# GpSimd mixes the rows for v and r of a time-mixing layer, and TensorE multiplies them once

## The reference

```
xs = jnp.pad(x, ((0, 0), (1, 0), (0, 0)))[:, :-1]        # the row of one step earlier
xk = x * time_mix_k + xs * (1.0 - time_mix_k)
xv = x * time_mix_v + xs * (1.0 - time_mix_v)
xr = x * time_mix_r + xs * (1.0 - time_mix_r)
K, V, R = xk @ Wk.T, xv @ Wv.T, xr @ Wr.T
wkv = _wkv(W, U, K, V)                                    # a scan over the 256 steps
output = (jax.nn.sigmoid(R) * wkv) @ Wo.T
```

## Time and profile before

| | us |
|---|---|
| time, median of 3 runs | 412.81 (411.13 to 414.19) |
| the profiled execution | 414.23 |
| its span | 412.2 |
| TensorE busy with matmuls | 353.9 |
| VectorE busy | 283.1 |
| ScalarE busy | 234.3 |
| GpSimd busy | 186.0 |

### The profile page before, as it was taken

One profiled execution on the slowest core, in us unless ns is written; L12 is line 12 of the kernel. 1 busy time (PEld: TensorE's weight loads), 2 busy tenths in 40 slices (PEclk: granted clock), 3 DMA queues, 4 the chain that ended last, 5 costly groups with the idle time before them and its releaser, 6 DMA issues.

```text
span 412.2 us, 6923 instructions
## 1 busy us (share of the span) xinstructions
PE 353.9 (86%) x2435; PEld 219.1 (53%) x2435; DVE 283.1 (69%) x669; ACT 234.3 (57%) x417; POOL 186.0 (45%) x339
## 2 busy tenths in 40 slices
PE   6869999899999999999888989797885587999930
PEld 2444545466475755747464756363633353788820
DVE  5694676774958669485985477789887864455633
ACT  2756796857759497585537334959757440333300
POOL 4001635747283562897561402500039107777750
PEclk9868999999999999999999999999998766999985
DMA  8400000000000000000000001900010011455346
GB/s 231 125 0 2 2 0 2 1 2 2 2 0 2 2 0 2 2 2 0 2 2 0 2 0 40 338 3 1 0 57 0 0 53 25 108 154 153 97 137 204
DMA packets 18035, 18.07 MB, mean 44 GB/s; under 512 B 2937, under 2 KB 14234, under 8 KB 17746
## 3 DMA queue, kind: packets, MB, share of 16 engines
q1 hardware_dynamic: 14930, 12.91, 10.6%
q0 software_dynamic: 1440, 2.90, 2.7%
q10 hardware_dynamic: 1632, 1.84, 1.3%
HBM read 12.12 MB, written 5.62 MB: 43 GB/s over the span
## 4 chain that ended last, share of the span: by engine, by line
PE 58%; DVE 15%; ACT 12%; issue 6%; DMA 4%; POOL 3%; POOLq 0%; ACTq 0%; DVEq 0%
PE at_av L258 9%; PE at_sim L241 8%; PE at_misc L278 6%; PE mo_y L2028 6%; PE at_misc L207 5%; PE mo_h L2016 4%; PE at_misc L202 4%; ACT at_attn L462 3%; PE at_misc L222 3%; DVE at_attn L615 2%; PE at_misc L271 1%; ACT at_sq_v L440 1%; PE mi_yf L1059 1%; PE at_sim L1059 1%; DVE ah_lm_stats L1121 1%
## 5 line engine op out<-in xcount | busy, mean ns | idle before, releaser
L615 DVE TENSOR_TENSOR at_attn<-at_sim,at_attn 128x1024 f32<-128x1024 f32 x64 | 75.3, 1218 | 41.8 <-ACT at_attn L462 41.4
L462 ACT ACTIVATE at_attn<-at_sim 128x1024 f32<-128x1024 f32 x64 | 62.2, 1029 | 36.8 <-PE at_sim L241 36.4
L766 POOL TENSOR_TENSOR at_osq<-at_ob 128x512 f32<-128x512 f32 x32 | 35.1, 1100 | 67.5 <-ACT at_ob L470 66.9
L258 PE MATMUL at_av<-at_attn,at_v_raw 128*64 128x256 f32 x512 | 64.1, 393 | 0.4 <-DVE at_v_raw L606 0.4
L258 PEld LDWEIGHTS at_av<-at_attn,at_v_raw 128*64 128x64 f32 x512 | 34.6, 139 | 25.2 <-issue 8.7
L1273 POOL TENSOR_SCALAR mi_at_lane<-mi_raised_lanes,mi_lane_of,mi_number 128x128 f16<-128x128 f32 x20 | 18.8, 955 | 58.0 <-DVE mi_lane_of L1786 58.0
L241 PE MATMUL at_sim<-at_q,at_k 32*128 32x256 f32 x512 | 41.1, 410 | 4.1 <-DVE at_attn L615 2.2
L2067 ACT ACTIVATE mo_hT<-mo_h,mo_b 128x320 f32<-128x320 f32 x32 | 16.3, 528 | 37.6 <-PE mo_h L2016 23.3
L207 PE MATMUL at_misc<-at_w_kv,at_xnT 128*128 128x512 f32 x64 | 33.9, 629 | 2.4 <-ACT at_sq_v L440 2.2
L241 PEld LDWEIGHTS at_sim<-at_q,at_k 32*128 32x128 f32 x512 | 25.3, 188 | 18.9 <-issue 9.3
L278 PE MATMUL at_misc<-at_w_out,at_ob 128*128 128x128 f32 x256 | 30.1, 276 | 0.0
(11 more groups left out here) (305 smaller groups left out, 677.5 us busy)
## 6 DMA issues: line engine op xcount, KB each, us to landing
mo_w<-in_L_ffn_w SPq DMA_DIRECT2D x16, 256.0 KB, 3.0
mo_answers<-mo_zero SPq DMA_DIRECT2D x2, 1024.0 KB, 8.9
mo_got<-mo_answers SPq DMA_DIRECT2D x6, 256.0 KB, 4.4
mo_rows<-ro_rows SPq DMA_DIRECT2D x4, 276.0 KB, 2.3
at_w_kv<-in_L_attn_Wkv ACTq DMA_DIRECT2D x1, 640.0 KB, 4.6
x_res<-in_L_attn_tokens SPq DMA_DIRECT2D x2, 256.0 KB, 6.1
at_w_out<-in_L_attn_Wout SPq DMA_DIRECT2D x1, 512.0 KB, 9.2
mo_b<-in_L_ffn_b SPq DMA_DIRECT2D x1, 512.0 KB, 4.8
```

The lines of the kernel that those rows point to most:

```text
L258: last = mm(av[e * DV:(e + 1) * DV, half * T:(half + 1) * T], v_raw[b % 2][:, j, h * DV:(h + 1) * DV], attn[(2 * Q + half) % 4][:, e, j, : ...
L462: nc.scalar.activation(attn[n % 4][:, :, :, :].rearrange("p e j t -> p e (j t)"), sim[half][:, :, :], ACT.Relu).then_inc(relu_ready, 1)
L615: v.tensor_tensor(r, sim[half][:, :, :], r, ALU.mult).then_inc(attn_ready, 1)
L766: g.tensor_tensor(osq[b % 2][:, 2 * n:2 * n + 2, :], o, o, ALU.mult).then_inc(osq_ready, 1)
```

## The change

For chunks 0 to 2, v and r are mixed before the multiplication: GpSimd subtracts the earlier rows from the rows (`step`), multiplies the difference by the mixing factor of the channel, and adds the earlier rows, for v and then for r, into the SBUF tiles `mixed_v` and `mixed_r`. TensorE multiplies each mixed tile once by the unmixed weights, and waits for `mixed_ready` first. Chunk 3 goes on as before, and k in all chunks. The unmixed weights of v and r therefore stay in place, and their mixed version goes to new tiles `w_new`. GpSimd's list gets the mixing of chunk 0 ahead of the blanks, of chunk 1 behind the ones, and of chunk 2 behind the constants. GpSimd waits for the chunk's rows (`xwT_ready`), and before it overwrites a mixed tile for the projection that read it (`v_done`, `r_done`); it waits for its own instructions through `link` where one reads what the one before wrote.

```diff
--- before.py
+++ after.py
@@ -861,6 +861,7 @@
 
 MIN_P = -1e38
 MIX = ("k", "v", "r")
+MIXED = ("v", "r")
 
 
 class WkvInputs:
@@ -872,6 +873,7 @@
 
         self.w = {m: sb("w_" + m, [P, P]) for m in ("k", "v", "r", "o")}
         self.w_old = {m: sb("w_old_" + m, [P, P]) for m in MIX}
+        self.w_new = {m: sb("w_new_" + m, [P, P]) for m in MIXED}
         self.ident, self.minus = sb("ident", [P, P]), sb("minus", [P, P])
         self.cols, self.keep = sb("cols", [P, 5]), sb("keep", [P, 3])
         self.minus_u = sb("minus_u", [P, 1])
@@ -896,7 +898,8 @@
             g.tensor_scalar(self.w_old[m][:, :], self.w[m][:, :], self.keep[:, n:n + 1], None, ALU.mult).then_inc(self.prepared, 1)
         pool.wait_ge(self.prepared, 6)
         for n, m in enumerate(MIX):
-            g.tensor_scalar(self.w[m][:, :], self.w[m][:, :], self.cols[:, 2 + n:3 + n], None, ALU.mult).then_inc(self.prepared, 1)
+            own = self.w_new[m] if m in MIXED else self.w[m]
+            g.tensor_scalar(own[:, :], self.w[m][:, :], self.cols[:, 2 + n:3 + n], None, ALU.mult).then_inc(self.prepared, 1)
 
 
 EXPERTS, EXPERT_HIDDEN, CAPACITY = 8, 512, 320
@@ -1187,7 +1190,10 @@
 
 
         w, w_old, minus, cols, minus_u = wkv.w, wkv.w_old, wkv.minus, wkv.cols, wkv.minus_u
+        w_new = wkv.w_new
         decay, xwT = ahead.decay, ahead.xwT
+        step = sb("step", seq)
+        mixed = {m: sb("mixed_" + m, seq) for m in MIXED}
         pp = sb("pp", [P, NB, T + 1])
         sums = sb("sums", [P, 2, NB, T + 1])
         u = [sb(f"u{i}", seq) for i in range(4)]
@@ -1252,7 +1258,7 @@
         mask_ready, counts_done, routed, meta_ready = sem("mask_ready"), sem("counts_done"), sem("routed"), sem("meta_ready")
         above_ready, lanes_ready, last_lanes, found = sem("above_ready"), sem("lanes_ready"), sem("last_lanes"), sem("found")
         centred, rwc_ready = sem("centred"), sem("rwc_ready")
-        chain = sem("chain")
+        chain, pool_chain, mixed_ready = sem("chain"), sem("pool_chain"), sem("mixed_ready")
 
         def formed(c):
 
@@ -1298,9 +1304,27 @@
             g.memset(eps[:, :], LN_EPS).then_inc(consts, 1)
             g.memset(pp[:, :, 0:1], MIN_P).then_inc(consts, 1)
             g.memset(sums[:, :, :, 0:1], 0.0).then_inc(consts, 1)
+            link = Chain(pool, pool_chain)
+
+            def mix(c):
+
+                now, before = xwT[c % 2][:, :, 1:T + 1], xwT[c % 2][:, :, 0:T]
+                pool.wait_ge(xwT_ready, c + 1)
+                link(g.tensor_tensor(full(step), now, before, ALU.subtract))
+                for m, used in zip(MIXED, (v_done, r_done)):
+                    n = MIX.index(m)
+                    if c:
+                        pool.wait_ge(used, c)
+                    link(g.tensor_tensor(full(mixed[m]), full(step), cols[:, 2 + n:3 + n].unsqueeze(2).to_broadcast(seq), ALU.mult))
+                    g.tensor_tensor(full(mixed[m]), full(mixed[m]), before, ALU.add).then_inc(mixed_ready, 1)
+
+            pool.wait_ge(wkv.prepared, 9)
+            pool.wait_ge(ahead.prepared, 3)
+            mix(0)
             moe.make_blanks(g)
             g.memset(ones[:, :], 1.0).then_inc(consts, 1)
             g.memset(one_row[:, :], 1.0).then_inc(consts, 1)
+            mix(1)
             pool.wait_ge(moe.consts_loaded, 16 * 9)
             g.tensor_scalar(centring[:, :], moe.ident[:, :], -1.0 / P, None, ALU.add).then_inc(consts, 1)
             g.tensor_copy(tri[:, :], moe.tri32[:, :]).then_inc(consts, 1)
@@ -1311,6 +1335,7 @@
             g.tensor_scalar(number[:, :], tokens[:, :], 1.0, None, ALU.add).then_inc(consts, 1)
             g.tensor_copy(rows[:, :, TOKEN], tokens[:, :]).then_inc(consts, 1)
             pool.wait_ge(consts, 13)
+            mix(2)
             for r in range(FINAL):
                 pool.wait_ge(routed, r + 1)
                 for k in range(2):
@@ -1349,8 +1374,15 @@
                 ahead.transpose_f(pe, c, xt)
 
             def project(m, c, dst):
+                now = w_new[m] if m in MIXED else w[m]
                 mm(by_batch(dst), w_old[m][:, :], xwT[c % 2][:, :, 0:T], start=True, stop=False)
-                return mm(by_batch(dst), w[m][:, :], xwT[c % 2][:, :, 1:T + 1], start=False, stop=True)
+                return mm(by_batch(dst), now[:, :], xwT[c % 2][:, :, 1:T + 1], start=False, stop=True)
+
+            def project_mixed(m, c, dst):
+                if c == LAST:
+                    return project(m, c, dst)
+                pe.wait_ge(mixed_ready, 2 * c + MIX.index(m))
+                return mm(by_batch(dst), w[m][:, :], full(mixed[m]), start=True, stop=True)
 
             def project_k(c):
                 pe.wait_ge(wkv.prepared, 9)
@@ -1368,12 +1400,12 @@
                 pe.wait_ge(xwT_ready, c + 1)
                 if c:
                     pe.wait_ge(v_used, c)
-                project("v", c, v_bank).then_inc(v_done, 1)
+                project_mixed("v", c, v_bank).then_inc(v_done, 1)
 
             def project_r(c):
                 if c:
                     pe.wait_ge(rw_ready, c)
-                project("r", c, r_bank).then_inc(r_done, 1)
+                project_mixed("r", c, r_bank).then_inc(r_done, 1)
 
             def gate(c, k, bank):
                 pe.wait_ge(ahead.xfT_ready, c + 1)
```

## The result

| | before | changed |
|---|---|---|
| median of 9 runs each, us | 412.19 | 416.67 |
| ratio, 95% interval | 1 | 1.0099 (1.0063 to 1.0136) |
| profiled execution, us (span) | 414.23 (412.2) | 416.67 (414.7) |

What follows compares the result with a forecast made beforehand. It took TensorE's chain of waits, with v's projection on it twice, as the bound, VectorE about a microsecond behind in chunk 1. Terms 3.9 + 1.7 + 0.95 = 6.55 on 412.8 gave 419.4 us, range 413.9 to 423.5.

Steps and rivals of the forecast that it cites:

- The mechanism: Chunk 1: GpSimd's mixing and VectorE's two-SBUF-operand instructions wait for each other whole, making total 4.7 us late.
- the starved GpSimd: Rival: VectorE keeps GpSimd out until chunk 1's total ends, v is mixed late, 3.4 us lost, 416.2; chance 0.13.
- within 1%: Outcome class 408.7 to 416.9 us: first rival, most of the second and the forecast's low end; chance 0.27.
- a VectorE that isn't held: Rival: GpSimd's reads leave VectorE room, the 1.5 us come out, 411.3; chance 0.12.
- the clock that stays low: Rival: TensorE's clock stays low through chunk 2's down projection or the routing, 9 us and more; chance 0.15.
- GpSimd's price: Each 128x512 mixing instruction takes 1.27 us, 1.13 after a wait; low end 1.04.
- the count for the low end: Chunk 1 with 1.04 us per GpSimd instruction, step going first: total 3.45 late; sum 2.75, 415.6 us.
- the signs: Chunk 1's scans, past and total each 1.7 to 2.3 us, total ending near 271, clock under 1.00 between 270 and 280.
- What is late next: Behind chunk 1's total, ScalarE's copy of the transposed rows comes late, so TensorE's gate matmul starts 3.9 us later.
- The clock: Gate matmul and subtraction run at 1.2 instead of 2.4 GHz: 1.7 us more, from 0 to 2.69 beyond that.
- Chunk 2: r's addition waits under scaled, then holds q; rw ends late, so the chain's addition starts 0.95 us late.
- What the change removes: Six fp32 matmuls in chunks 0 to 2, two on the chain: 0.86 and 0.62, together 1.5 us if nothing else moved.

Runs made afterwards that it cites:

- experiment 4: Kernel before, with chunk 1's five mixing instructions added as GpSimd memsets of a spare tile, TensorE waiting for them and projecting twice: 410.25 us, ratio 0.9975.
- 1: Changed kernel with GpSimd still mixing and TensorE waiting, but v and r again projected with two matmuls by the scaled weights: 416.55 us, ratio 1.0084.
- experiment 7: Changed kernel with chunks 1 and 2 mixed in VectorE's gaps and their v projected later on TensorE; run twice: 410.48 and 410.86 us, ratio 0.9963 both times.
- the second of 8: Version with mixing in VectorE's gaps and v projected later, but v and r projected with two matmuls as in the kernel before: 412.19 us, ratio 1.0007.
- experiment 3: Three runs, each mixing only one chunk on GpSimd, the others as in the kernel before: chunk 0 411.31, chunk 1 418.01, chunk 2 413.84 us.
- chunk 2 alone: Only chunk 2 mixed on GpSimd and multiplied once, chunks 0 and 1 as in the kernel before: 413.84 us, ratio 1.0033.
- chunk 0 alone: Only chunk 0 mixed on GpSimd and multiplied once, chunks 1 and 2 as in the kernel before: 411.31 us, ratio 0.9992.
- experiment 2: Changed kernel without any mixing: v and r of chunks 0 to 2 multiply the unmixed rows once: 413.96 us, ratio 1.0060.
- 5: Kernel before, no GpSimd mixing, with v of chunks 1 and 2 projected behind the following down projection and output product: 412.82 us, ratio 0.9997.
- 6: Kernel before with v of chunks 1 and 2 projected later and the filler matmuls ahead of chunk 3's transposes taken out: 412.86 us, ratio 1.0004.
- chunk 1 alone: Only chunk 1 mixed on GpSimd, chunks 0 and 2 as in the kernel before: 418.01 us, ratio 1.0153.

## Why the prediction was right, and where its sizes were off

**The mechanism.** Right, and shown: the same neighbour without reads holds nothing (experiment 4), the mixing without the saved matmuls loses the same (1), and out of VectorE's way it loses nothing (7, and the second of 8 with ratio 1.0007). The time alone wouldn't have shown it: 416.67 is nearer to the starved GpSimd's 416.2 than to my 419.4, and by 0.2 us it lies in the class "within 1%", to which I gave 0.27. The rivals of a VectorE that isn't held and of a starved GpSimd are out by the lockstep of the first two fences, and the clock that stays low (9 us and more) by the down projection's 2.69 and the 5.26 at the end.

The condition was too narrow. I wrote of VectorE's instructions with two operands in SBUF, but the row that I took the hold from (213.83), like the one of 1.03 in experiment 3, is a TENSOR_SCALAR of one tensor (L71). That instructions with one operand in PSUM run free was assumed; the 1.26 of the running maximum shows it.

**GpSimd's price.** The term that was off. I took 1.27, drawn from the smaller shapes; alone the step and the multiplication took 1.04 and the addition 1.18, so the slope between 32 and 128 columns doesn't hold up to 512, and the square of the earlier trace rows was the better row. The estimate from the Trainium skill, "GPSIMD Engine Reference", section "Performance versus the Vector engine", 1.12, lay between them; the trace agrees with it better than with mine. The two additions ended 0.97 and 0.99 behind the scan that released them, where I had 1.13; VectorE's turns I had at 0.55 and 1.09, measured 0.55 and 1.07. The step also came ahead of the first scan, as in the count for the low end. So total was 3.53 late, not 4.7; that count, with 1.04, gave 3.45. Hence the signs came out smaller than I had named: scans of 1.4 and 1.5 in place of 1.7 to 2.3, past of 1.56, and a total that isn't lengthened (1.23). TensorE didn't wait for GpSimd anywhere in the stretch.

**What is late next.** The gate matmul was 3.10 later, not 3.9. I named ScalarE's copy of the transposed rows; the chain goes through the up matmul, which waits for a VectorE product behind total. The two end close together: the copy at 269.41 (268.83 and 0.58), the up matmul at 269.81. By the copy alone the gate would have been some 2.75 later; the other 0.35 are the clock's, since the up matmul ran at half speed.

**The clock.** 1.09 in place of 1.7: gate 1.73 and subtraction 1.08, together 2.81 where 0.86 each was due; with the 0.35 of the up matmul it is 1.44. The down projection ran at full speed (2.69). But it isn't all the change's own: in experiment 4, where nothing on VectorE was held, the granted clock from 266 to 270 was 0.66, and the addition of chunk 2 stood at 23.54, 1.6 behind the kernel before. With chunk 2 alone mixed, where every engine's list up to there does what that of before does, it was 0.67 and 23.49. So how much of the 1.44 the late total caused stays open.

**Chunk 0.** Nothing, as predicted, with 0.35 of cover left in the changed kernel.

**Chunk 2.** 0.79 (4.98 less 4.19) where I had 0.95, but in the changed kernel it came another way. k of chunk 2 took 1.79 and 1.71 at the lower clock, ScalarE's inversion and with it scaled came late, and r's addition (290.15, 1.18) was over before scaled began at 291.58. The hold I described is real where the clock is up (chunk 2 alone, experiment 3).

**The sum.** 4.19 and 0.79 make 4.98, another 0.28 comes after, 5.26 in the profile against 6.55: 0.80 less at the gate, 0.61 less clock behind it, 0.16 less in chunk 2. The 0.28 is a net figure that I had not in the sum: at the start of the experts this profile ran matmuls at the lower clock (2.08 for eight of 128x128 where before has 1.16) and was up to 8.5 late, and it got most of that back at the end, where VectorE's additions wait 4.4 us for data and not 7.8. The runs' medians differ by 4.5. Without attention's scatter the profiles part clearly: from the release to the end of the span they take 159.3 to 160.5 us where chunk 1's scans are free (before, chunk 0 alone, experiments 2, 4, 5, 6 and the second of 8), 164.5 to 165.4 where they are held (changed, 1, chunk 1 alone), and 157.6 and 157.1 in experiment 7. What the change removes I priced at 1.5 on the chain; that gain exists (1.22 in experiment 2), and I was right that it is lost in a wait here. That v and r of chunk 2 could count later, ahead of the routing's transposes, I did not see.

**Open.** The parts of experiment 3 add to more (1.8%) than the whole change (1.0%); their intervals are wide enough for it, and I have no row that explains it. The profile of chunk 2 alone, the slowest of its 12 runs, has the same slow start of the experts as the changed kernel's and 163.7 us from the release to the end, so its span is no price for chunk 2.

## What to carry to other kernels

Before work goes to an idle GpSimd, list what VectorE does in those microseconds: where it reads two operands in SBUF (and in a TENSOR_SCALAR of one), a GpSimd instruction that reads SBUF takes turns with it, and where VectorE is the bound each turn is added to the path. In this kernel five instructions cost 3.53 us. The cure is a wait on VectorE's own progress that puts the GpSimd work into its gaps, with the consumer moved back in its in-order list at the same time; here the first without the second lost 1.4%. A matmul saved is worth something only where the list behind it is late: look further than the chain's next join, to what stands behind it on the same engine.

## What the runs showed of the hardware

- The hold reaches scans and instructions of 4 columns, and a TENSOR_SCALAR with one operand in SBUF: a scan pair of 1.32 becomes 2.77, 0.17 becomes 1.03. Scans with one operand in PSUM (1.26 with and without GpSimd) and the statistics L1124 (0.84 both ways) are not held. A memset of GpSimd (0.95 each, five of them) holds none.
- A held instruction shows no idle time in the profile. Here it was found by comparing durations of the same shape.
- The granted clock differs between executions of nearly the same list: from 266 to 270 us it was 1.00 before, 0.66 in experiment 4 and 0.67 with chunk 2 alone mixed, at a cost of 1.6 us at the next addition. Differences of a few tenths of a per cent need many runs here.
